# Row maxima subtracted in four wide products per tile, and the zero-padded copies of x taken after the query's copy

## What is computed

```python
h = _L0_tok_ref(x, W_h, b_h, W_o, b_o, W_r, b_r)        # silu MLP plus linear
h = h + _L0_attn_ref(_layernorm(h), Wq, Wk, Wv, W_out, b_out)
h = h + _L0_ffn_ref(_layernorm(h), w_freq_real, w_freq_imag, bias)

# in _L0_attn_ref
energy = einsum('bqhd,bkhd->bhqk', q, k) / sqrt(e)
attn = softmax(energy, axis=-1)
```

## Time and profile before

| | |
|---|---|
| median of 3 runs | 140.39 us (140.27 to 140.44) |
| profiled execution | 140.08 us |
| its span | 138.2 us |
| PE busy | 132.4 us, 96% |
| DVE busy | 111.3 us, 81% |
| ACT busy | 85.6 us, 62% |
| POOL busy | 95.0 us, 69% |
| TensorE's clock | granted at full speed nearly throughout (mean 0.997) |

### The profile page before, as it was taken

The page is one execution under the profiler, slowest core; times in us unless marked ns, Lnnn a source line. Parts: engine busy times, 40 slices in busy tenths (PEclk is TensorE's granted clock), DMA queues, the critical chain, the costliest instruction groups (busy, mean ns, idle before and its releaser), DMA issues.

```text
span 138.2 us, 6119 instructions
## 1 busy us (share of the span) xinstructions
PE 132.4 (96%) x2443; PEld 111.5 (81%) x2443; DVE 111.3 (81%) x337; ACT 85.6 (62%) x245; POOL 95.0 (69%) x186
## 2 busy tenths in 40 slices
PE   6799999999999999999999999999999999999991
PEld 2489999999988787978878889888788897887650
DVE  5695497679978579898898898988989989879671
ACT  5467475478868585864947748659476485662410
POOL 3384699998547274678687696886876968674750
PEclk9999999999999999999999999999999999999998
DMA  4577100120000020120312303213123031121012
GB/s 68 157 176 230 55 0 0 14 33 2 0 0 5 0 24 5 19 52 14 64 38 24 62 0 62 48 16 66 39 24 60 2 62 46 15 57 47 5 38 76
DMA packets 24508, 5.89 MB, mean 43 GB/s; under 512 B 20384, under 2 KB 24224, under 8 KB 24480
## 3 DMA queue, kind: packets, MB, share of 16 engines
q1 hardware_dynamic: 24192, 5.37, 18.5%
q10 hardware_dynamic: 288, 0.13, 0.4%
HBM read 2.35 MB, written 2.10 MB: 32 GB/s over the span
## 4 chain that ended last, share of the span: by engine, by line
PE 87%; DVE 4%; ACT 4%; issue 1%; ACTq 1%; POOL 0%; DVEq 0%; POOLq 0%
PE bank L1067 11%; PE bank L973 10%; PE bank L1053 7%; PE bank L1109 6%; PE bank L1129 6%; PE bank L978 5%; PE bank L1162 5%; PE bank L1116 5%; PE bank L1097 4%; PE bank L967 3%; PE bank L1175 3%; PE bank L1080 2%; PE bank L1166 2%; PE bank L1133 2%; PE bank L1184 2%; PE bank L1154 2%
## 5 line engine op out<-in xcount | busy, mean ns | idle before, releaser
L830 DVE TENSOR_REDUCE bank<-bank 128x4 f32<-128x256 f32 x64 | 22.8, 425 | 6.8 <-ACT pT L377 6.3
L377 ACT ACTIVATE pT<-bank 128x256 f32<-128x256 f32 x64 | 19.4, 393 | 2.6 <-PE bank L1080 2.5
L1067 PEld LDWEIGHTS bank<-qT,xzT 32*128 32x128 f32 x512 | 15.7, 186 | 2.7 <-issue 2.7
L1067 PE MATMUL bank<-qT,xzT 32*128 32x64 f32 x512 | 17.9, 276 | 0.0
L702 DVE TENSOR_TENSOR hid_lo<-bank,hid_hi 128x512 fp32r<-128x512 f32 x16 | 11.0, 686 | 7.3 <-ACT bank L342 7.1
L588 POOL TENSOR_TENSOR side_lo<-sideT,side_hi 128x256 fp32r<-128x256 f32 x14 | 10.2, 729 | 7.9 <-ACT sideT L388 7.9
L549 POOL TENSOR_SCALAR xblk<-xh,parity_sb 128x128 f32<-128x128 f32 x32 | 11.6, 375 | 5.8 <-PE bank L1116 4.6
L372 ACT ACTIVATE maxT<-bank 128x128 fp32r<-128x128 f32 x16 | 4.4, 278 | 17.7 <-PE bank L1089 17.7
L599 POOL TENSOR_TENSOR on_lo<-onT,on_hi 128x256 fp32r<-128x256 f32 x14 | 10.3, 738 | 7.1 <-ACT on_hi L392 6.9
L557 POOL TENSOR_TENSOR hb_all<-h_all,bout_bc 128x256 f32<-128x256 f32 x16 | 11.6, 734 | 3.9 <-ACT h_all L346 3.9
L341 ACT ACTIVATE hid_hi<-bank 128x512 fp32r<-128x512 f32 x16 | 9.6, 599 | 5.0 <-PE bank L967 5.0
(11 more groups left out here) (170 smaller groups left out, 380.8 us busy)
## 6 DMA issues: line engine op xcount, KB each, us to landing
out<-y SPq DMA_DIRECT2D x16, 128.0 KB, 1.7
xblk<-xh SPq DMA_DIRECT2D x32, 32.0 KB, 2.3
wo_raw<-in_W_o SPq DMA_DIRECT2D x1, 512.0 KB, 3.9
wout_raw<-in_W_out SPq DMA_DIRECT2D x1, 256.0 KB, 3.0
fr<-in_wr SPq DMA_DIRECT2D x1, 256.0 KB, 4.6
fi<-in_wi SPq DMA_DIRECT2D x1, 256.0 KB, 4.7
minus_raw<-in_minus_rows SPq DMA_DIRECT2D x1, 128.0 KB, 2.1
bout_bc<-in_b_out SPq DMA_DIRECT2D x1, 128.0 KB, 4.1
```

The lines of the kernel that those rows point to most:

```text
L377: nc.scalar.activation(pT[:, j, :], bank[j][:, D:2 * D], ACT.Exp).then_inc(exp_done, 1)
L830: nc.vector.tensor_reduce(rowmax[:, j, :], bank[j][:, 0:D].rearrange("p (h k) -> p h k", k=TOK), AX_X, ALU.max).then_inc(max_done, 1)
L1067: pe.matmul(bank[j][:, at0:at0 + TOK], xzT[t % 3][rows32, 2 * half + b, :, :].rearrange("p e k -> p (e k)"), qT[t % 3][rows32, half, TOK * ...
```

## The change

1. `take_max` runs four products of 256 columns for a tile instead of eight of 128. `minus_rows` loses its dimension of halves, so that the same 32 x 128 weights serve both halves; what separates the halves is now the moving side: maxT gets two copies, [128, 2, 128], each multiplied by a new column of `parity` that keeps the rows of its half's heads. So `copy_max` is two ACT instructions with a scale from SBUF instead of one without. `keyed_done` counts four for a tile as before; `take_max` waits for both copies.
2. In ACT's step `copy_xzT(i+3)` moves from behind `copy_xT` to the very end, behind `exponent` and `copy_q`. It waits for `x_lo_set`, which is set by then in the loop.
3. DVE's `split_x` no longer waits for xzT but for `x_hi` (from tile 2 on), and `split_x(2)` moves ahead of the first maxima in the start of the pipeline. PE's `turn_x` waits for xzT of the tile before too, as its copies now read bank 4 last.

```diff
-    minus_rows = np.where((r[:, None, None] % 32 < 8) & (r[:, None, None] % 4 == head_of[None]), -1.0, 0.0).astype(np.float32)
+    parity = (np.stack([r // HD % 2, r // HD % 2, r // TOK, r // TOK, r % 4 // 2, r % 4 // 2], 1)
+              == [0, 1, 0, 1, 0, 1]).astype(np.float32)
+    minus_rows = np.where((r[:, None] % 32 < 8) & (r[:, None] % 2 == r[None, :] // TOK), -1.0, 0.0).astype(np.float32)
...
-        maxT = sb("maxT", [P, P], F32R)
+        maxT = sb("maxT", [P, HALF, P], F32R)
...
             def copy_xzT(t):
+                act.wait_ge(x_lo_set, t + 1)
                 for e in range(2):
...
             def copy_max(t):
                 act.wait_ge(max_turned, t + 1)
-                nc.scalar.activation(maxT[:], bank[MAX_BANK][:, 0:P], ACT.Copy).then_inc(max_copied, 1)
+                for half in range(HALF):
+                    nc.scalar.activation(maxT[:, half, :], bank[MAX_BANK][:, 0:P], ACT.Copy,
+                                         scale=parity[:, 4 + half:5 + half]).then_inc(max_copied, 1)
...
                 if i + 3 < T:
                     copy_xT(i + 3)
-                    copy_xzT(i + 3)
                 if i < WHOLE_ON:
                     lead_on(i)
                 if i + 1 < T:
                     exponent(i + 1)
                 if i + 3 < T:
                     copy_q(i + 3)
+                    copy_xzT(i + 3)
...
             def split_x(t):
-                dve.wait_ge(xzT_copied, 2 * (t + 1))
+                if t < 2:
+                    dve.wait_ge(xzT_copied, 2 * (t + 1))
+                dve.wait_ge(xT_copied, t + 1)
...
+            split_x(2)
             dve.wait_ge(zeros_set, 3)
             for j in range(QUADS):
                 maximum(0, j)
             split_max(0)
-            split_x(2)
...
-                pe.wait_ge(max_copied, t + 1)
+                pe.wait_ge(max_copied, HALF * (t + 1))
                 if t == 0:
                     pe.wait_ge(minus_set, 1)
-                for half in range(HALF):
-                    for j in range(QUADS):
-                        rows32 = slice(32 * j, 32 * j + 32)
-                        last = pe.matmul(bank[j][:, D + half * P:D + (half + 1) * P], minus_rows[rows32, half, :],
-                                         maxT[rows32, :], start=False, stop=(half == HALF - 1), skip_group_check=True)
-                        if half == HALF - 1:
-                            last.then_inc(keyed_done, 1)
+                for j in range(QUADS):
+                    rows32 = slice(32 * j, 32 * j + 32)
+                    pe.matmul(bank[j][:, D:2 * D], minus_rows[rows32, :],
+                              maxT[rows32, :, :].rearrange("p h q -> p (h q)"),
+                              start=False, stop=True, skip_group_check=True).then_inc(keyed_done, 1)
...
                 if t >= 1:
                     pe.wait_ge(q_copied, t)
+                    pe.wait_ge(xzT_copied, 2 * t)
```

More of the change, by code:

```diff
@@ L44, in launch_constants @@
     head_blocks = (r[:, None] // HD == r[None, :] // HD).astype(np.float32)
-    parity = (np.stack([r // HD % 2, r // HD % 2, r // TOK, r // TOK], 1) == [0, 1, 0, 1]).astype(np.float32)
-    head_of = 2 * np.arange(HALF)[:, None] + np.arange(P)[None, :] // TOK
-    minus_rows = np.where((r[:, None, None] % 32 < 8) & (r[:, None, None] % 4 == head_of[None]), -1.0, 0.0).astype(np.float32)
+    parity = (np.stack([r // HD % 2, r // HD % 2, r // TOK, r // TOK, r % 4 // 2, r % 4 // 2], 1)
+              == [0, 1, 0, 1, 0, 1]).astype(np.float32)
+    minus_rows = np.where((r[:, None] % 32 < 8) & (r[:, None] % 2 == r[None, :] // TOK), -1.0, 0.0).astype(np.float32)
     pair_ones = (r[:, None] // TOK == np.arange(32)[None, :] // HD).astype(np.float32)
@@ L75, in audio_tower_kernel @@
         blocks = sb("blocks", [P, P])
-        parity = sb("parity_sb", [P, 4])
+        parity = sb("parity_sb", [P, 6])
         cosine = sb("cosine_sb", [P, D])
@@ L138, in audio_tower_kernel @@
         qT = [sb(f"qT{i}", [P, HALF, P]) for i in range(3)]
-        minus_raw = sb("minus_raw", [P, HALF, P])
-        minus_rows = sb("minus_rows_sb", [P, HALF, P], F32R)
+        minus_raw = sb("minus_raw", [P, P])
+        minus_rows = sb("minus_rows_sb", [P, P], F32R)
         pair_ones = sb("pair_ones_sb", [P, 32])
         max_terms = sb("max_terms", [P, QUADS, 32], F32R)
-        maxT = sb("maxT", [P, P], F32R)
+        maxT = sb("maxT", [P, HALF, P], F32R)
         pT = sb("pT", [P, QUADS, D])
```

## The result

The changed kernel takes 143.57 us in the median of six runs (143.09 to 143.97), the kernel before, run beside it, 140.41 us (140.10 to 140.62). The ratio is 1.022, with a 95% interval of 1.020 to 1.025: **slower by 3.2 us**. The forecast was 142.1 us and slower; the sign and the mechanism hold, the loss is nearly twice the one worked out. The profiled execution took 143.09 us with a span of 141.0 us.

A forecast was written before the change was run, and what follows sets the result against it. PE, busy 96% of the span, was taken as the bound: +3.42 us of waits for xzT and -1.65 us from take_max give +1.77 us on 140.39, so 142.1 us; 8-in-10 range 140.9 to 144.0 us.

The forecast's parts named there:

- the sign and the mechanism: Whole kernel: slower, as PE's new wait for xzT (+3.42 us) outweighs the saving in take_max (-1.65 us).
- PE is the bound, and the wait at its step's head is not covered: Head of PE's steps: PE, busy 96%, waits 0.27 us a step for the moved xzT copies, +3.42 us in sum.
- The pair of copies: ACT's two xzT copies behind copy_q: start 0.26 us after copy_q starts and span 0.87 us.
- The exponent: ACT's exponent: starts about 0.39 us after take_max's first product.
- Take_max: PE's subtraction of maxima: four wide products save 0.12 us a tile (bounds 0.08 and 0.14), -1.65 us in sum.
- the 0.21 us from the query's last product to `weigh`: PE at the step seam: a full 256-column product's distance to the next array shape, taken for take_max's one round.
- The second copy of maxT costs nothing: ACT's copy_max: two scaled copies end 0.65 us after the first starts instead of 0.28, hidden from PE, cost nothing.
- lead_on ahead of xzT gives nothing: ACT's lead_on and exponent no longer stand behind xzT; PE waits for neither in steady steps, so no gain.
- the copies are hidden: Rival at the step seam: the copies end by the time weigh does, only the saving is left, 138.7 us; chance 0.08.
- cancel the saving: Rival at the step seam: a wait near 0.13 us a step equals take_max's saving, 140.4 us; chance 0.07.
- A second wait for POOL: Rival in steady steps: ACT's later copies make POOL's side_lo and on_lo late, 143.3 us for 0.1 us; chance 0.09.
- The start: Pipeline start: split_x(2) fits DVE's idle gap before the first maximum; smaller cast and minus_rows load give nothing.

The follow-up runs named there:

- e3: The changed kernel with PE's wait for qT and xzT moved behind turn_side and turn_max; 140.73 us, ratio 1.0035 to the kernel before.
- e4: The changed kernel with take_max's four products cut to 128 columns, so the second half of the heads is not subtracted; one time, 144.58 us.
- e7: The kernel before with one spare scaled ACT copy of the turned maxima ahead of maxT; 141.65 us, ratio 1.010.
- e1: Wide products only: the changed kernel with the xzT copies, the waits and split_x(2) in their old places; 143.43 us, ratio 1.022.
- e8: e1 with POOL's normalize (xh) ahead of add_bias (h2b); 143.82 us, ratio 1.023 to the kernel before.
- e5: e3 with three buffers and three semaphores for y instead of two; 139.96 us, ratio 0.998 to the kernel before.

## Why the prediction was right, and where its size was off

*PE is the bound, and the wait at its step's head is not covered.* Right. Forecast 0.27 us in steps 2 to 13, measured 0.26 in twelve rows, and e3 takes it away by moving that wait alone. The pair of copies spanned 0.83 us, not 0.87, and started 0.28 after copy_q. The exponent starts 0.40 us after take_max's first product, where 0.39 was named.

*Take_max.* **This is the term that was mis-sized**: 0.12 us a tile forecast, with bounds of 0.08 and 0.14; measured 0.055, below both. The step that failed is the row it was read from: the 0.21 us from the query's last product to `weigh`, taken for a round of four products of 32 rows. A product of the whole array did not stand for a round in four row groups: the query's last product lasts 0.28 us, the round 0.38, and the next shape starts only 0.07 before either ends. e4 gives the terms: 0.25 for a round of 128 columns, 0.06 for 128 more, 0.11 for a second round. Over steps 1 to 12 the error is 12 x 0.065 = 0.8 us, which covers the distance of 0.7 us between the forecast +1.77 and the 2.5 us that the span lost behind its start; the wait, 0.01 a step shorter than forecast, takes 0.1 back.

*The second copy of maxT costs nothing, and lead_on ahead of xzT gives nothing.* Each is right in the changed kernel: e3's step is exactly before's less 0.055. But they are right only together. The copies put 0.34 us into ACT's chain to on_hi and the exponent, and the move takes the 0.72 us of xzT out of it. In the old order a second copy costs 0.11 (e7) or, with both scaled, 0.21 us a step (e1). I priced the copy against take_max, side_lo and on_lo, and missed the exponent, DVE's maxima and h behind it, where only 0.07 us were to spare, and xh, which ended at the start of turn_x already.

*The rivals.* That the copies are hidden, or cancel the saving, is out: twelve waits. A second wait for POOL, the rival on the far side, did not come in the changed kernel: on_lo is there 0.4 us early. It shows in e1 and e8, where it is not what sets the step.

*The start.* split_x(2) in DVE's gap cost nothing. The 0.4 us of slower first products were not foreseen. TensorE's clock rose later in that execution, and that this is not the change's is likely, not shown. Of the 0.4 us, 0.3 are left at tile 2's query copy. With the 2.5 us behind it the span is 2.8 us longer, the profiled execution 3.0 us, and the medians are 3.2 us apart; the last 0.2 us are within the spread of the times.

## What to carry to other kernels

Before an instruction is moved behind another on its engine, find the wait that names it on the consumer's queue, and count what stands between that wait and the first real use: here three turning products, enough to hide the whole loss, stood behind the wait and not ahead of it. A copy that is "off the path" has as many deadlines as it has successors; follow each successor to the bound engine, since e1 and e8 lost 2.5 us to a loop through ACT, DVE and back to PE. A wait that the profile shows need not be the one that sets the step: e8 took one away and another grew by as much. Look for the last wait in the loop, the one that starts a fixed time after its releaser in every step. Parts of a change that each lose can only be judged together: wide products alone lost 2.2%, the move alone 2.1%, both with the wait behind the turning products in every step and a third output buffer won 0.5%.

## What was not expected of the hardware

The store of one tile (128 KB, 1.7 us in the median) can be over a microsecond late at the very end: in e3 the last y waited 1.18 us for it. In that stretch an instruction load (16 KB) lies beside the stores. The DMA queues of e3 from 133 to 138 us:

```profile
q1 hardware_dynamic: 432, 0.39, 23.3%
q8 instruction: 1, 0.02, 1.5%
```

The twelve traces hold 192 stores of a tile. Six of them took over 3 us (3.15 to 3.88): that of tile 13 in e1, e3, e4, e5 and e8, and that of tile 12 in the repeat of before. In each of the six an instruction load starts 1.06 to 1.17 us after the store's issue, and for none of the other 186 does one start between 0 and 1.2 us after it. Where the load starts 1.24 to 1.7 us after the issue, the store takes 1.7 to 2.1 us. So the two go together; how the load holds the store up is open, and no run moved it. It cost time only where the last y then waited, in e1, e3, e4 and e8 (1.2 to 1.8 us).

Four products of 32 rows with 256 columns each, in four row groups, cost 0.06 us more than four with 128 columns (0.31 against 0.25), so a second half of the columns was nearly free beside a second round with its loads (0.11).
